# Two PSUM banks instead of one for the key norms, two instead of three for the value transposes, four instead of three in the FFN

## The reference

```python
x = x + attn_a(layernorm(x))     # q = z @ wq @ fcq_w + fcq_b, k and v alike; 16 heads of 64
x = x + ffn(layernorm(x))        # gelu(x @ w1 + b1) @ w2 + b2, 1024 -> 4096 -> 1024
x = x + attn_b(layernorm(x))     # qkv = x @ w_qkv; the same 16 heads of 64
x = x + ffn(layernorm(x))
```

## Time and profile before

| what | us |
|---|---|
| median of the 2 runs shown | 3521.49 |
| the two runs | 3470.99 and 3571.99 |
| profiled execution, its own time | 3387.1 |
| its span, slowest core (7) | 3385.7 |
| spans of its 8 cores | 3356.1 to 3385.7 |

### The profile page before, as it was taken

One profiled execution on the slowest core, in us unless ns is written; L12 is line 12 of the kernel. 1 busy time (PEld: TensorE's weight loads), 2 busy tenths in 40 slices (PEclk: granted clock), 3 DMA queues, 4 the chain that ended last, 5 costly groups with the idle time before them and its releaser, 6 DMA issues.

```text
span 3385.7 us, 33887 instructions; the slowest of 8 cores (3356.1 to 3385.7 us)
## 1 busy us (share of the span) xinstructions
PE 2625.6 (78%) x10664; PEld 915.0 (27%) x10664; DVE 1120.9 (33%) x1570; ACT 1602.9 (47%) x1800; POOL 64.3 (2%) x122
## 2 busy tenths in 40 slices
PE   5456878687875599998847778787888773999889
PEld 1111222122221243343213322222222221334334
DVE  4543544444534021210243235444444422112110
ACT  2247989798930313212212239894898700320311
POOL 0000000000000000000000000000000000000000
PEclk8656999799987899999868889999899996999999
DMA  4000000000004725224011110001000018432532
GB/s 113 0 1 7 5 4 5 2 4 4 5 12 71 125 38 100 50 50 75 1 19 19 19 26 4 4 5 27 3 5 4 4 20 144 89 77 64 106 69 50
DMA packets 36263, 121.01 MB, mean 36 GB/s; under 512 B 7936, under 2 KB 12032, under 8 KB 26880
## 3 DMA queue, kind: packets, MB, share of 16 engines
q0 software_dynamic: 20832, 97.53, 16.7%
q1 hardware_dynamic: 12384, 12.93, 1.3%
q10 hardware_dynamic: 2880, 8.39, 0.7%
HBM read 203.50 MB, written 8.39 MB: 63 GB/s over the span
## 4 chain that ended last, share of the span: by engine, by line
PE 57%; ACT 16%; DVE 11%; DMA 7%; issue 6%; another core or an unknown queue 3%; DVEq 0%; ACTq 0%; SPq 0%; POOLq 0%; POOL 0%
ACT POOL L479 13%; PE PS_A L704 5%; PE PS_B L704 5%; PE PS_A L731 5%; PE PS_B L731 5%; PE PS_A L418 5%; DMA POOL<-w_h 4%; PE PS_D L731 3%; PE PS_C L494 3%; PE PS_D L494 3%; DVE sstat L139 2%; PE PS_C L498 2%; DVE SCR L139 2%; PE PS_A L911 2%
## 5 line engine op out<-in xcount | busy, mean ns | idle before, releaser
L479 ACT ACTIVATE POOL<-PS_A,ebias 128x1024 bf16<-128x1024 f32 x512 | 570.4, 1114 | 101.8 <-PE PS_C L498 38.8
L479 ACT ACTIVATE POOL<-PS_B,ebias 128x1024 bf16<-128x1024 f32 x512 | 570.3, 1114 | 21.2 <-PE PS_C L498 6.8
L704 PE MATMUL PS_A<-BIG,POOL 128*128 128x512 bf16 x1024 | 256.7, 396 | 156.4 <-DMA POOL<-w_h 131.9
L143 ACT ACTIVATE BIG<-PS_A,bcols 128x512 bf16<-128x512 f32 x144 | 98.9, 687 | 557.2 <-PE PS_A L704 543.6
L418 PE MATMUL PS_A<-BIG,POOL 64*128 64x512 bf16 x512 | 196.0, 383 | 101.4 <-ACT POOL L479 99.7
L704 PE MATMUL PS_B<-BIG,POOL 128*128 128x512 bf16 x1024 | 249.3, 388 | 0.0
L418 PE MATMUL PS_B<-BIG,POOL 64*128 64x512 bf16 x512 | 196.0, 383 | 60.2 <-ACT POOL L479 58.6
L139 DVE SCALAR_TENSOR_TENSOR X<-PS_A,bcols,X 128x512 f32<-128x512 f32 x56 | 42.0, 750 | 589.2 <-PE PS_A L731 463.5
L139 DVE RECIPROCAL PF<-SCR 33x512 f32<-33x512 f32 x64 | 214.1, 3345 | 66.2 <-DMA SCR<-PF 66.2
L494 PE MATMUL PS_C<-POOL 128*65 128x512 bf16 x512 | 212.6, 415 | 29.0 <-DVE SCR L139 29.0
L494 PE MATMUL PS_D<-POOL 128*65 128x512 bf16 x512 | 206.9, 404 | 6.1 <-ACT POOL L479 6.1
(11 more groups left out here) (153 smaller groups left out, 3023.0 us busy)
## 6 DMA issues: line engine op xcount, KB each, us to landing
POOL<-w_h POOLq DMA_DIRECT2D x64, 1024.0 KB, 8.6
POOL<-w_h POOLq DMA_DIRECT2D x2, 8192.0 KB, 55.9
X<-xT SPq DMA_DIRECT2D x4, 1024.0 KB, 22.4
X<-xT ACTq DMA_DIRECT2D x4, 1024.0 KB, 25.3
BIG<-POOL SPq DMA_DIRECT2D x64, 64.0 KB, 1.9
POOL<-wqkv_kv POOLq DMA_DIRECT2D x16, 256.0 KB, 4.3
POOL<-wqkv_q POOLq DMA_DIRECT2D x16, 256.0 KB, 3.5
yT<-X SPq DMA_DIRECT2D x16, 256.0 KB, 2.4
```

The costliest lines, as they stand in the source:

```text
L143: return p.inc(getattr(nc.scalar, name)(*a, **k), "act", 1)
L479: nc.scalar.activation(psb, PSx[:, :], AF.Exp, bias=ebias[:, c:c + 1], scale=0.125),
L704: tt = nc.tensor.matmul(PSx[:, ucoff:ucoff + 512], wg[:, dc * 512 + j * 128: dc * 512 + j * 128 + 128], BIG2[:, hoff(dc):hoff(dc) + 512], ...
```

## The change

Three places, with no arithmetic added or removed:

- `emit_knorm` writes the row sums alternately to PS_D and PS_E, and a matmul waits for the maximum before the last one (`mx[sl - 2]`) instead of the last one. Its entry waits of ScalarE for all TensorE work now hold in every turn, and the memory of the previous turn (`kn_prev`) is gone.
- `emit_vtranspose` uses the two banks of PS_C only: rounds 0 and 2 the first, rounds 1 and 3 the second. Round 2 waits for round 0's copy and round 3 for round 1's. The entry waits for all VectorE and all ScalarE work now hold in every turn.
- `emit_qnorm2_and_ebias` uses PS_D and PS_E instead of the two banks of PS_A. The FFN's down-projection rotates through four banks, PS_E being the new one.

```diff
-        def emit_vtranspose(vts_off, cpair, entry=False):
+        def emit_vtranspose(vts_off, cpair):
+            p.wait(nc.tensor, "dve")
             p.wait(nc.tensor, "act")
-            if entry:
-                p.wait(nc.tensor, "dve")
-            banks = [PS_C[:, 0:512], PS_C[:, 512:1024], PS_D[:, 0:512]]
+            round_ev = {}
+            round_eng = {}
             for r4 in range(4):
-                bi = r4 % 3
-                g = vt_bank_ev.get(bi)
-                if g is not None:
-                    p.wait(nc.tensor, g[0], g[1])
+                boff = (r4 % 2) * 512
+                if r4 >= 2:
+                    p.wait(nc.tensor, round_eng[r4 - 2], round_ev[r4 - 2])
...
         def emit_knorm(cpair, sq_off):
-            if cpair == 0:
-                p.wait(nc.scalar, "te")
-                kn_prev.clear()
+            p.wait(nc.scalar, "te")
             p.wait(nc.scalar, "dve")
+            psl = [PS_D[0:1, 0:512], PS_E[0:1, 0:512]]
...
-                g = tmm.get(sl - 2) or kn_prev.get("t%d" % (sl + 2))
-                if g is not None:
-                    p.wait(nc.scalar, "te", g)
+                if sl >= 2:
+                    p.wait(nc.scalar, "te", tmm[sl - 2])
                 sq = sop("activation", ksq, kc_ap, AF.Square)
                 p.wait(nc.tensor, "act", sq)
-                gm = mx.get(sl - 1) or kn_prev.get("m3")
-                if gm is not None:
-                    p.wait(nc.tensor, "dve", gm)
+                if sl >= 2:
+                    p.wait(nc.tensor, "dve", mx[sl - 2])
-                tmm[sl] = p.inc(nc.tensor.matmul(PS_E[0:1, 0:512],
-                                                 ones_b[:, 0:1], ksq,
-                                                 start=True, stop=True),
+                tmm[sl] = p.inc(nc.tensor.matmul(psl[sl % 2], ones_b[:, 0:1],
+                                                 ksq, start=True, stop=True),
                                 "te", 1)
...
         def emit_qnorm2_and_ebias(sq_off):
-            psl = [PS_A[0:1, 0:512], PS_A[0:1, 512:1024]]
+            psl = [PS_D[0:1, 0:512], PS_E[0:1, 0:512]]
...
         # emit_ffn
-                    if uc < 4 and obank_ev.get(uc % 3) is not None:
-                        p.wait(nc.tensor, "dve", obank_ev[uc % 3])
+                    if uc < 4 and obank_ev.get(uc % 4) is not None:
+                        p.wait(nc.tensor, "dve", obank_ev[uc % 4])
...
-                obanks = [(PS_A, 512), (PS_B, 512), (PS_D, 0)]
+                obanks = [(PS_A, 512), (PS_B, 512), (PS_D, 0), (PS_E, 0)]
...
-                    PSx, coff = obanks[fo % 3]
-                    if obank_ev.get(fo % 3) is not None:
-                        p.wait(nc.tensor, "dve", obank_ev[fo % 3])
+                    PSx, coff = obanks[fo % 4]
+                    if obank_ev.get(fo % 4) is not None:
+                        p.wait(nc.tensor, "dve", obank_ev[fo % 4])
```

More of the change, by code:

```diff
@@ L295, in emit_layernorm_exp @@
             return out
-        vt_bank_ev = {}
-        def emit_vtranspose(vts_off, cpair, entry=False):
+        def emit_vtranspose(vts_off, cpair):
+            p.wait(nc.tensor, "dve")
             p.wait(nc.tensor, "act")
-            if entry:
-                p.wait(nc.tensor, "dve")
-            banks = [PS_C[:, 0:512], PS_C[:, 512:1024], PS_D[:, 0:512]]
+            round_ev = {}
+            round_eng = {}
             for r4 in range(4):
-                bi = r4 % 3
-                g = vt_bank_ev.get(bi)
-                if g is not None:
-                    p.wait(nc.tensor, g[0], g[1])
+                boff = (r4 % 2) * 512
+                if r4 >= 2:
+                    p.wait(nc.tensor, round_eng[r4 - 2], round_ev[r4 - 2])
                 for j in range(4):
                     kt = r4 * 4 + j
-                    psv = banks[bi][:, j * 64:(j + 1) * 64].bitcast(BF16)
+                    psv = PS_C[:, boff + j * 64: boff + (j + 1) * 64].bitcast(BF16)
                     src = POOL[:, vts_off + kt * 128: vts_off + kt * 128 + 128]
@@ L327, in emit_vtranspose @@
                         v = sop("activation", da, sa, AF.Identity)
-                vt_bank_ev[bi] = ("dve" if r4 % 2 == 0 else "act", v)
+                round_ev[r4] = v
+                round_eng[r4] = "dve" if r4 % 2 == 0 else "act"
             return p.cnt["dve"]
-        kn_prev = {}
         def emit_knorm(cpair, sq_off):
-            if cpair == 0:
-                p.wait(nc.scalar, "te")
-                kn_prev.clear()
+            p.wait(nc.scalar, "te")
             p.wait(nc.scalar, "dve")
+            psl = [PS_D[0:1, 0:512], PS_E[0:1, 0:512]]
             tmm = {}
@@ L339, in emit_knorm @@
             for sl in range(4):
-                off = sq_off if sl % 2 == 0 else MB + 8192
-                ksq = POOL[:, off:off + 512]
+                ksq = POOL[:, (sq_off if sl % 2 == 0 else MB + 8192):
+                           (sq_off if sl % 2 == 0 else MB + 8192) + 512]
                 kc_ap = KAR[:, cpair * T + sl * 512: cpair * T + sl * 512 + 512]
-                g = tmm.get(sl - 2) or kn_prev.get("t%d" % (sl + 2))
-                if g is not None:
-                    p.wait(nc.scalar, "te", g)
+                if sl >= 2:
+                    p.wait(nc.scalar, "te", tmm[sl - 2])
                 sq = sop("activation", ksq, kc_ap, AF.Square)
                 p.wait(nc.tensor, "act", sq)
-                gm = mx.get(sl - 1) or kn_prev.get("m3")
-                if gm is not None:
-                    p.wait(nc.tensor, "dve", gm)
-                tmm[sl] = p.inc(nc.tensor.matmul(PS_E[0:1, 0:512],
-                                                 ones_b[:, 0:1], ksq,
-                                                 start=True, stop=True),
+                if sl >= 2:
+                    p.wait(nc.tensor, "dve", mx[sl - 2])
+                tmm[sl] = p.inc(nc.tensor.matmul(psl[sl % 2], ones_b[:, 0:1],
+                                                 ksq, start=True, stop=True),
                                 "te", 1)
                 p.wait(nc.vector, "te", tmm[sl])
-                mx[sl] = vop("reduce_max", S_KSL(sl), PS_E[0:1, 0:512],
-                             axis=AX.X)
+                mx[sl] = vop("reduce_max", S_KSL(sl), psl[sl % 2], axis=AX.X)
             vop("reduce_max", S_KMAX(cpair), sstat[0:1, 16:20], axis=AX.X)
-            kn_prev["t2"] = tmm[2]
-            kn_prev["t3"] = tmm[3]
-            kn_prev["m3"] = mx[3]
         def emit_qnorm2_and_ebias(sq_off):
@@ L741, in emit_ffn @@
                                  b_b2(fo), xs, ALU.add, ALU.add)
-                    obank_ev[fo % 3] = ev[fo]
+                    obank_ev[fo % 4] = ev[fo]
                     if store_out:
@@ L822, in build @@
                 p.wait(nc.tensor, "act")
-                emit_vtranspose(OA_VTS, c, entry=(c == 0))
+                emit_vtranspose(OA_VTS, c)
             kv_done = p.cnt["dve"]
@@ L931, in build @@
                 emit_knorm(c, OB_SQ)
-                emit_vtranspose(OB_VTS, c, entry=(c == 0))
+                emit_vtranspose(OB_VTS, c)
             kvb_done = p.cnt["dve"]
```

## The result

The changed kernel takes 3361.2 us (median of 11 runs), the kernel before 3432.2 us in the 10 runs taken with it. A part of the executions of either kernel has one die (four of the eight cores) at a lower clock and takes up to 260 us longer; they are left out of the comparison, and the two runs that stood ahead of the prediction (3470.99 and 3571.99) were such executions. The ratio of the others is **0.9913, 95% interval 0.9900 to 0.9925**: 29 us faster, between 25 and 34. That is within 2%.

The account below looks back on a forecast made before the run. Bound in stage a by a chain of short dependent steps, in stage b by dense matmuls and a gap for norm and transposes. Gains 12.8 + 7.2 = 20 us, 3387.1 to 3367.1 us; range 3354 to 3560.

Parts of the forecast that it names:

- waits that only changed in form: Norm: ScalarE's entry wait for TensorE is covered by waits for the same matmuls' evacuations; 0 us.
- dense part of stage b: Stage b, next keys to next first row sum: no term in the sum; only the gap before it was costed.
- The level of 3501: Whole kernel: the same 0.6% gain taken off 3521.49, the median of the runs shown, gives 3501 us.
- Key norm, two banks: Stage a key norm: fourth row sum starts 2.38 us earlier in each of 8 turns, 19.0 us gained.
- Transposes in stage a: Stage a: with two banks the keys' evacuation starts 0.77 us later in each of 8 turns, 6.2 us lost.
- Entry wait hidden in stage a: Transposes' entry, stage a: the wait for all of VectorE costs nothing; ScalarE's value evacuations hide it by 3 us.
- Rival 1: Stage b: the clock moves with the shorter gap; 13 us more gained (3354), or only 7 gained (3380); chance 0.15.
- The sign on the clock: Stage b: the prediction is wrong if the granted clock leaves 0.80 by more than 0.05.
- The other two signs of being wrong: Norm and transposes: wrong if sums still stand 1.58 us apart, or the entry wait costs over 2 us.
- The rule on bank cycling: PSUM banks: alternating PS_D and PS_E would swing the clock and lengthen stage b's slow part, giving 3380 us.
- FFN and query norm at nothing: FFN's fourth down-projection bank and query norm on PS_D and PS_E: no idle time or waits to remove, 0 us.
- Rival 2: Key norm: the bank was not what it waited for; only costs stay, 16.6 us slower, 3404 us; chance 0.05.

Follow-up runs that it names:

- with fillers: Idle-time matmuls, never read, added in stage b's gap: on the changed kernel ratio 0.9870, stage b 188.70 us; on the kernel before stage b 206.80 us.
- the second comparison on another chip: The changed kernel again, unaltered, against the kernel before on another chip: two comparable runs, 3369.3 and 3371.1 us, ratio 0.994.

## Why the prediction was right or wrong

*The mechanisms forecast were right, the size of the gain was too small: 20 us forecast, 13 to 25 as the likeliest case's own range, 29 (25 to 34) by the ratio, 25.05 in the two stages. Two terms put at nothing failed: the waits that only changed in form (1.1 us in stage a, 0.8 in stage b) and the dense part of stage b, which the sum left out (3.5 us of granted clock). The level of 3501 failed too.* Step by step:

- **Key norm, two banks, 19.0 us in stage a: right.** Sum 0 to the value matmul 2.88 us against 2.89 worked out.
- **Transposes in stage a, a loss of 6.2 us: right.** Alone they cost 6.5, and taking them back brought 6.3.
- **Entry wait hidden in stage a: right.** Without it the stage is the same 125.10 us. In stage b it was said to come 0.26 us after kmax and to make the gap 7.15 us, and that is the figure. The gaps of the eight turns together fell from 65.85 to 58.88 us, 7.0 us; 7.2 were worked out (only the last turn missed, 8.76 for 8.41). Without the wait they fell by another 7.7, to 51.2.
- **"Waits that only changed in form: 0": the step that failed in stage a.** The waits are fulfilled, but a fulfilled wait behind the blocking one isn't free. It was 1.1 us in stage a (shown with the kernel before, same banks) and, by 0.11 us a turn (15.70 against 15.59 with fillers), 0.8 in stage b.
- **The dense part of stage b left out of the sum: the step that failed there.** It shrank from 17.48 to 16.88 us, 4.2 us over seven turns. 0.8 of them are the waits, and the remaining 3.5 granted clock: the turns of 0.80 are gone, and with the clock at 1.00 in the dense parts of both kernels these differ by 0.11 us alone. Rival 1 said that the clock could move either way, with 0.15 for it and 13 us if the fall stayed away. It was there, a quarter of the size: the fall still comes in every turn. Why this gap loses less of the dense part than the longer one stays open. The runs show what it lost each time, and no rule that would have forecast it.
- **The sign on the clock** came out at its edge. The prediction counted itself wrong if the granted clock of stage b left 0.80 by more than 0.05. Over the whole stage it's 0.84 or 0.85 on the eight cores after the change and about 0.81 before. The other two signs of being wrong, sums 1.58 us apart and an entry wait of over 2 us, didn't come (the wait costs 1.1 us a turn in stage b, 7.15 against 6.0 without it).
- **The rule on bank cycling**, weighed in the prediction, isn't borne out here: alternating two banks left stage b at a granted clock of 0.86 a turn instead of 0.80 to 0.86. The Trainium skill ("TensorE: Matmul & The Clock Gate", section "A second HAM failure mode: psum-queue depth-cycling") describes a kernel whose cycling through PSUM banks makes the clock swing, and the prediction read from it a longer slow part. The slow part got shorter.
- **FFN and query norm at nothing: right**, 1.0004.
- **Rival 2's costs** were met by the run that has only the transposes: 19 us slower where 16.6 were worked out, the difference again in the dense part.
- **The level of the time was wrong.** 3501 stood on the median of the two runs shown ahead of it, neither of which belongs to the comparison. On the profiled execution's scale the forecast was 3367.1 and the changed kernel's median is 3361.2. The wide range held it, but at its lower end; the base that the profile gave was the one to use.

Not settled: the ratio says 29 us, the stages 25. 25 is the lower end of the interval, the FFN and query norm show nothing (though 4 us would lie at their interval's edge), and the second comparison on another chip points to less than 25. No run shows a further gain.

## What to carry to other kernels

A serial chain through one PSUM bank can be read off the timeline and re-timed to 0.1 us with the durations that are already there. But the buffer one takes for it comes from somewhere: here the lost third transpose bank and a blanket wait cost 19 us (the ratio 1.0057 where they came alone), and using a bank that was free at that moment (the second bank of PS_B) instead, with a narrower wait, kept both. Where a gap between dense matmuls changes, read the granted clock of the dense part too: shortening the gap by 0.6 us a turn (6.6 against 7.15) once brought 0.8 us of the 4.8 expected in the stage, because the matmuls behind it got slower by nearly as much.

## What the runs showed of the hardware

- A wait that was fulfilled long ago costs time if it's emitted behind the one that blocks: 0.11 us on TensorE and 0.06 us on ScalarE (square to sum 0.77 instead of 0.89, evacuation to square 0.14 instead of 0.20). On ScalarE it was enough to put it ahead of the blocking one. On TensorE it was left out, and its place alone wasn't tried.
- The clock lost in a gap isn't a smooth function of the gap. Gaps of 7.9, 7.15, 6.6, 6.0 and 5.7 us had dense parts of 17.5, 16.9, 17.4, 17.1 and 16.7 us, in the last two as a mix of turns between 15.6 and 17.9. (The first has 0.11 us of waits in it.)
- Fillers in a gap gave the dense part behind it the full clock (15.6 us at 1.00) even where they began after the fall: the clock came back within the gap. But then they are slow themselves and hold up what stands behind them. Five of 128x512 behind the last sum took 1.25 us in one or two turns of eight of the changed kernel, and 1.9 to 2.3 in the others and in every turn of the kernel before. Placed ahead of the sums they took no more than 1.24 us in any turn, and the gap stayed at 5.5 to 5.65 us in most.
